# A four-layer gated transformer block on one core: the weight strips, router pieces and layer-norm scales of the second expert layer in another order

## The chip, the core and the metric

The kernel runs on one core of one Trainium2 chip. A core has five engines that work side by side and wait for each other through semaphores: TensorE (PE, matrix products), VectorE (DVE), ScalarE (ACT), GpSimd (POOL) and SyncE (SP, which here only starts DMAs). The time is the device time of one launch in microseconds (us). The profile is one execution of the same program with the hardware profiler on.

## What is computed

Input x is 8 sequences of 128 tokens with 128 features, so 1024 tokens. Four layers follow each other; each adds a gated attention and a gated feed-forward part. The change touches the feed-forward part of the second layer (layer 1 in the code), a mixture of 8 experts:

```python
nx = _ln(x, ln_g, ln_b)
probs = softmax(nx @ router_w)                     # 8 experts, the top 2 kept, w normalised
h1 = gelu(einsum('th,ehf->etf', nx, up_W) + up_b)  # H 128, F 512
s0 = gelu(_ln(einsum('etf,efg->etg', h1[[0,4]], spec0_W) + spec0_b, ln0_g, ln0_b))
t1 = gelu(einsum('etf,efg->etg', h1[[1,5]], spec1a_W) + spec1a_b)      # 512 -> 256
s1 = _ln(einsum('etg,egf->etf', t1, spec1b_W) + spec1b_b, ln1_g, ln1_b) # 256 -> 512
s2 = gelu(einsum('etf,efg->etg', h1[[2,6]], spec2_W) + spec2_b)
h2 = h1 with experts 0,4 <- s0; 1,5 <- s1; 2,6 <- s2
out_e = einsum('etf,efh->eth', h2, down_W) + down_b
y = einsum('eth,te->th', out_e, w) + x
```

All 8 experts run on all tokens; the router's weights are multiplied in at the end. Experts 0, 4, 1 and 5 have a layer norm inside; 2 and 6 have an inner product without one; 3 and 7 have none.

## The kernel before

**Numbers.** Every large product is made of three matmuls on split operands: each operand is written as a high part and a low part (value minus high part), and the product is high times high, high times low, low times high (`mm3`). So every weight and every hidden tile has to be split before TensorE can use it.

**Weights.** SyncE loads a unit's weights into `RAW`. They are split in strips of 128x512 (a `split` piece): VectorE writes the high part `WH` (`high_part`, the CAST in L936), then GpSimd writes the low part `WL` (`low_part`, L607). An expert has one strip for its up weights, four for its inner weights and one for its down weights. TensorE waits for the last strip of an area at the first product that uses it. `RAW` holds one expert's weights, so the DMA for the next expert's area starts when the strips that lay there have their low parts.

**Hidden tiles.** A piece `up`, `spec1a`, `spec2` or `turn` ends in one bank of PSUM (128x512). ScalarE reads it twice, into `G` (L750) and into the high part `H1h` or `H2h` (L752); VectorE then writes the low part `H1l` or `H2l` (L1082). There are four slots of `G`.

**Layer norms.** `spec0` (expert 0, 4) and `spec1b` (expert 1, 5) give one token tile each, four tiles to a half of the tokens (h0, h1). VectorE takes the tile's moments out of PSUM (`tile_stats`: BN_STATS L1030, BN_AGGR L1031, variance L1032), GpSimd raises the variance to -0.5 (L617), VectorE writes the scaled tile `SN` (`tile_scale`, L1038). TensorE then transposes `SN` (`turn`, L1499); the first turn of a half waits for all four scales of that half.

**Ring.** Six PSUM banks are used in a ring by all pieces but `down`: TensorE starts a piece when the reader of the piece six before it is through. Two more banks hold the `down` results.

**Router.** The router's work on VectorE is five `route` pieces of small instructions on 128x64 (L960 to L999). ScalarE has one exponential between parts 0 and 1. The result `WGS` is transposed by TensorE (`wgt`), copied by ScalarE into `WGT`, and spread over partitions (`spread`); `weigh` multiplies an expert's output by it (VectorE, L1017), and GpSimd adds it up (L625).

**Order.** `plan()` writes one list of pieces for the layer (`order[1]`), and every engine walks through this one list and does its own part of each piece, strictly in that order. `weave(a, b, c)` interleaves lists, each one step behind the list before it. So a piece's place in the list sets its place in the queue of VectorE, of GpSimd and of TensorE at once; an engine that waits for one piece does none of the later ones. In the list of before, a layer-norm expert's six strips for the next expert stand in its layer-norm phases (`new[:4]` and `new[4:]` for expert 0 and 4, `new[:3]` and `new[3:]` for 1 and 5), the five router pieces stand in expert 0's second half, and expert 0's `wgt` and `spread` pieces stand behind its down products. A scale stands one piece behind its moments, and the last scale of a half directly behind its moments.

## Time and profile before

| | |
|---|---|
| median of 3 runs | 790.73 us (788.05 to 791.43) |
| span of the profiled execution, first to last instruction | 791.2 us |
| its own time | not listed apart from the span |
| mean granted TensorE clock | 0.922 of full speed |
| the second layer's experts in the span | about 203 to 516 us |
| share of TensorE in the chain that ended last | 70% |

The page gives, for one execution, each engine's busy time, the waits and what ended them, and a timeline. A wait on TensorE is shown in brackets behind the instruction that ended it. PEclk is the granted clock: 1.00 stands for 2.4 GHz, 0.50 for 1.2 GHz. Line numbers are those of the kernel before.

### The profile page before, as it was taken

The numbers are of one execution on the slowest core, as the hardware profiler recorded it, in microseconds if no ns is written. First come the engines' busy times: TensorE is split into PE (matmuls) and PEld (weight loads), VectorE is DVE, ScalarE is ACT, GpSimd is POOL, SyncE is SP. The second block draws the span as 40 slices with busy tenths as digits, with TensorE's granted clock in tenths as the row PEclk, the third lists the DMA queues.
The fourth block names the chain that finished last, engine by engine and source line by source line (L and its number), as shares of the span: only waits on it lengthen the run. The fifth ranks groups of instructions, "written<-read, shape, count | busy, mean of one in ns | idle before, by whom it ended". The sixth has DMA issues, their size and how long they took to land.

```text
span 791.2 us, 10027 instructions
## 1 busy us (share of the span) xinstructions
PE 700.5 (89%) x3468; PEld 547.8 (69%) x3475; DVE 553.0 (70%) x1242; ACT 367.5 (46%) x647; POOL 209.9 (27%) x193
## 2 busy tenths in 40 slices
PE   5989997999898998797999797993759999789997
PEld 2779983889666766675777586771546888567775
DVE  4688766788578585656667735769874554588996
ACT  2334442434435737455275464721214442486673
POOL 5113107322132041124424311143002220214431
PEclk9589997999799999999999989986879999799999
DMA  5102003000001010202010200030000000001000
GB/s 134 39 27 58 2 4 114 31 1 1 1 14 67 3 38 1 68 0 80 14 68 14 66 1 0 1 97 0 1 0 1 1 1 1 27 27 28 1 1 27
DMA packets 27361, 20.97 MB, mean 27 GB/s; under 512 B 5409, under 2 KB 22571, under 8 KB 27311
## 3 DMA queue, kind: packets, MB, share of 16 engines
q1 hardware_dynamic: 26591, 20.29, 8.7%
q8 instruction: 28, 0.46, 0.3%
q14 instruction: 22, 0.18, 0.1%
q10 hardware_dynamic: 720, 0.04, 0.1%
HBM read 19.80 MB, written 0.52 MB: 26 GB/s over the span
## 4 chain that ended last, share of the span: by engine, by line
PE 70%; DVE 17%; issue 4%; ACT 4%; POOL 3%; DMA 1%; ACTq 0%; DVEq 0%; POOLq 0%
PE PS L1366 61%; PE PS L1563 4%; DVE H2l L1082 2%; PE PS L1448 2%; POOL WL L607 2%; ACT H1h L752 1%; DVE SN L1038 1%; PE PS L1499 1%; ACT G L750 1%; DVE WH L936 1%; DVE XN L910 1%; PE PS L1386 1%; DMA GW<-in_L_gate_T 1%; DVE ST L891 1%; POOL RSTD L617 1%
## 5 line engine op out<-in xcount | busy, mean ns | idle before, releaser
L607 POOL TENSOR_TENSOR WL<-RAW,WH 128x512 fp32r<-128x512 f32 (+2 forms) x76 | 95.4, 1272 | 186.9 <-DVE WH L936 186.9
L1082 DVE TENSOR_TENSOR H2l<-G,H2h 128x512 fp32r<-128x512 f32 x104 | 84.0, 822 | 59.7 <-ACT H2h L752 58.7
L1082 DVE TENSOR_TENSOR H1l<-G,H1h 128x512 fp32r<-128x512 f32 x80 | 63.3, 800 | 28.9 <-ACT H1h L752 28.1
L1366 PE MATMUL PS<-H1h,WH 128*128 128x512 f32 x146 | 60.9, 417 | 8.0 <-DVE H1l L1082 8.0
L750 ACT ACTIVATE G<-PS,UB 128x512 f32<-128x512 f32 x64 | 44.8, 700 | 42.4 <-PE PS L1366 38.1
L1366 PE MATMUL PS<-XTh,WH 128*128 128x512 f32 x128 | 55.3, 432 | 9.8 <-POOL WL L607 5.3
L600 POOL TENSOR_TENSOR RSTD<-VE,MHALF 128x4 f32<-128x4 f32 x18 | 19.3, 1072 | 166.5 <-DVE VE L900 166.5
L1366 PEld LDWEIGHTS PS<-V,ATT 77*128 77x128 f32 x512 | 62.5, 192 | 0.6
L625 POOL TENSOR_TENSOR XT<-XT,YW 128x512 f32<-128x512 f32 x24 | 34.8, 1448 | 106.0 <-DVE YW L1017 106.0
L769 ACT ACTIVATE ATT<-ATT 128x308 f32<-128x308 f32 x64 | 29.4, 460 | 71.3 <-DVE ATT L1152 71.0
L1366 PE MATMUL PS<-V,ATT 77*128 77x9 f32 x512 | 61.3, 247 | 0.0
L1144 DVE TENSOR_REDUCE MX<-PS 128x4 f32<-128x308 f32 x64 | 30.5, 477 | 43.6 <-PE PS L1366 42.9
L1366 PE MATMUL PS<-H1l,WH 128*128 128x512 f32 x146 | 58.6, 401 | 0.0
L1366 PE MATMUL PS<-H1h,WL 128*128 128x512 f32 x146 | 58.4, 400 | 0.0
L1366 PE MATMUL PS<-H2h,WH 128*128 128x512 f32 (+1 forms) x108 | 50.6, 469 | 5.6 <-issue 2.0
L1366 PE MATMUL PS<-XTl,WH 128*128 128x512 f32 x128 | 54.0, 422 | 0.0
L685 ACT ACTIVATE ATT<-PS 77x512 f32<-77x512 f32 (+5 forms) x76 | 38.2, 517 | 33.6 <-PE PS L1734 17.0
L1366 PE MATMUL PS<-XTh,WL 128*128 128x512 f32 x128 | 53.8, 420 | 0.0
L1366 PE MATMUL PS<-BDK,ATT 128*128 128x308 f32 x128 | 49.1, 466 | 1.6 <-issue 1.6
L750 ACT ACTIVATE G<-PS,FB 128x512 f32<-128x512 f32 x64 | 43.3, 698 | 13.9 <-PE PS L1366 13.8
L1366 PE MATMUL PS<-H2h,WL 128*128 128x512 f32 (+1 forms) x108 | 44.0, 408 | 0.0
L1366 PE MATMUL PS<-H2l,WH 128*128 128x512 f32 (+1 forms) x108 | 44.0, 407 | 0.0
(242 smaller groups left out, 1677.8 us busy)
## 6 DMA issues: line engine op xcount, KB each, us to landing
RAW<-in_L_ffn_spec_W SPq DMA_DIRECT2D x4, 1024.0 KB, 5.6
RAW<-in_L_ffn_w SPq DMA_DIRECT2D x16, 256.0 KB, 3.0
RAW<-in_L_ffn_up_W SPq DMA_DIRECT2D x8, 256.0 KB, 2.7
RAW<-in_L_ffn_down_W SPq DMA_DIRECT2D x8, 256.0 KB, 3.6
RAW<-in_L_ffn_spec1a_W SPq DMA_DIRECT2D x2, 512.0 KB, 4.3
RAW<-in_L_ffn_spec1b_W SPq DMA_DIRECT2D x2, 512.0 KB, 5.2
RAW<-in_L_ffn_wg SPq DMA_DIRECT2D x4, 176.0 KB, 2.7
RAW<-in_L_ffn_wu SPq DMA_DIRECT2D x4, 176.0 KB, 2.7
```

The source lines that it names most:

```text
L600: g.tensor_tensor(RSTD[:, c], VE[:, c], MHALF[:, c], ALU.pow).then_inc(rstd_ready, 1)
L607: g.tensor_tensor(lo, RAW[0:r["rows"], r["raw"] + s["c0"]:r["raw"] + s["c1"]], hi.bitcast(fp32), ALU.subtract).then_inc(lo_done, 1)
L617: g.tensor_tensor(RSTD[:, i:i + 1], VE[:, i:i + 1], MHALF[:, 0:1], ALU.pow).then_inc(trstd_ready, 1)
L625: g.tensor_tensor(y, y, YW[:, (d % 2) * HALF:(d % 2 + 1) * HALF], ALU.add).then_inc(y_added, 1)
L685: return s.activation(o, i, ACT.Copy)
L750: last = s.activation(G[:, k % 4, :], bank[:, :], func, bias=bias, scale=scale)
L769: s.activation(group(PB, g), group(SUB, g), ACT.Exp, scale=scale).then_inc(exp_done, 1)
L1082: v.tensor_tensor(lo, full, hi.bitcast(fp32), ALU.subtract).then_inc(split_done, 1)
L1144: v.tensor_reduce(MX[:, (g % 4) * GH:(g % 4 + 1) * GH], bank(g), AX.X, ALU.max).then_inc(max_done, 1)
L1366: return t_.matmul(o, l, r, start=start, stop=stop)
L1448: last = t_.transpose(o[0:rows, t * S:(t + 1) * S], SN[:, h, at:at + rows], ident[:, :])
L1563: last = t_.transpose(PS[3 + g % 3][0:KC, m * S:(m + 1) * S], group(PB, g)[:, m * KC:(m + 1) * KC], ident[:, :])
```

## The change

It does three things, all in the second layer's list and in VectorE's walk through it. (1) In experts 0 and 4 the next expert's strips are taken out of the layer-norm phases: one stays between the halves, two stand in the last turns and first down products, three beside the second half's down products. In experts 1 and 5 the strips that stood among `spec1b` stand before it or behind the turns. (2) Router parts 1 to 3 stand among expert 0's down products, part 4 in expert 1's first phase, and expert 0's `wgt` and `spread` pieces stand in expert 1, behind its `up` pieces and ahead of `spec1b`. (3) VectorE's scale of a tile stands two pieces behind its moments; ahead of the first turn of a half all outstanding scales are done.

```diff
@@ down_of
-        if e == 0 and h == 0:
+        if e == 0 and (h == 0 or layer == 1):
             return g
@@
+    first_weights = [piece("wgt", 1, 0, k, 0) for k in range(2)] + [piece("spread", 1, 0, h, 0) for h in range(2)]
@@ plan, the list of layer 1
         if e % 4 == 0:
-            o += weave(spec("spec0", 0, TH), up(e, 1), new[:4])
+            o += weave(spec("spec0", 0, TH), up(e, 1))
             k = route() if e == 0 else []
-            o += k[0:1]
-            o += weave(spec("spec0", 1, TH), spec("turn", 0, 4, buf=2, hi="act"), new[4:], k[1:])
-            o += weave(spec("turn", 1, 4, buf=3, hi="act"), down(e, 0), nxt[:2])
-            o += weave(nxt[2:], down(e, 1))
+            o += new[:1] + k[0:1]
+            o += weave(spec("spec0", 1, TH), spec("turn", 0, 4, buf=2, hi="act"))
+            o += weave(spec("turn", 1, 4, buf=3, hi="act"), down(e, 0), nxt[:2] + k[1:3], new[1:3])
+            o += weave(nxt[2:], down(e, 1), k[3:4] + new[3:])
         elif e % 4 == 1:
-            o += weave(spec("spec1a", 0, 2, buf=2, hi="act"), up(e, 1), new[:3])
-            o += weave(spec("spec1b", 0, TH), spec("spec1a", 1, 2, buf=3, hi="act"), new[3:])
+            if e == 1:
+                o += weave(spec("spec1a", 0, 2, buf=2, hi="act"), up(e, 1), k[4:] + new[:2]) + first_weights + new[2:4]
+            else:
+                o += weave(spec("spec1a", 0, 2, buf=2, hi="act"), up(e, 1), new[:4])
+            o += weave(spec("spec1b", 0, TH), spec("spec1a", 1, 2, buf=3, hi="act"))
             o += weave(spec("spec1b", 1, TH), spec("turn", 0, 4, buf=2, hi="act"), nxt[:2])
-            o += weave(spec("turn", 1, 4, buf=3, hi="act"), down(e, 0), nxt[2:3])
+            o += weave(spec("turn", 1, 4, buf=3, hi="act"), down(e, 0), nxt[2:3], new[4:])
             o += weave(nxt[3:], down(e, 1))
@@ VectorE's mixture
-                    ready, late = late, []
+                    at_once = kind == "turn" and i == 0
+                    for m in late[:len(late) if at_once else max(0, len(late) - 2)]:
+                        if m is not None:
+                            tile_scale(m)
+                    late = [] if at_once else late[-2:]
+                    late.append(s if kind in ("spec0", "spec1b") else None)
@@
                     elif kind in ("spec0", "spec1b"):
                         tile_stats(s)
-                        late = [s]
-                        if i == TH - 1:
-                            for m in ready:
-                                tile_scale(m)
-                            ready, late = [s], []
                     elif kind == "weigh":
                         weigh(s)
-                    for m in ready:
-                        tile_scale(m)
```

**The last scale of expert 0's second half.** VectorE before, from the moments of tile 3 of h1 (PS7 is its bank) on; `SN<-PS7` is the scale that the first turn of h1 waits for:

```order
L1030 BN_STATS ST<-PS7 128x6
L1031 BN_AGGR MV<-ST 128x2
L1032 TENSOR_SCALAR VE<-MV 128x1
L1038 TENSOR_SCALAR SN<-PS7,MV,RSTD 128x512
L1082 TENSOR_TENSOR H2l<-G,H2h 128x512
L936 CAST WH<-RAW 128x512
```

VectorE now, from the moments of the same tile:

```order
L1035 BN_STATS ST<-PS7 128x6
L1036 BN_AGGR MV<-ST 128x2
L1037 TENSOR_SCALAR VE<-MV 128x1
L1043 TENSOR_SCALAR SN<-PS3,MV,RSTD 128x512
L1092 TENSOR_TENSOR H2l<-G,H2h 128x512 x2
L1043 TENSOR_SCALAR SN<-PS7,MV,RSTD 128x512
L1092 TENSOR_TENSOR H2l<-G,H2h 128x512 x3
```

The scale stood directly behind the variance; now two `H2l` splits (of the turns of h0, tiles 2 and 3) stand between. The line numbers have moved with the code.

**Expert 1's inner strips.** VectorE before, at the end of expert 0's first half and ahead of its second; CAST `WH<-RAW` is a weight strip's high part (here inner strips 0, 1 and 2 of expert 1):

```order
L1082 TENSOR_TENSOR H1l<-G,H1h 128x512
L936 CAST WH<-RAW 128x512
L1082 TENSOR_TENSOR H1l<-G,H1h 128x512
L936 CAST WH<-RAW 128x512 x2
L960 COPY RT_60<-PS4 128x64
L961 TENSOR_REDUCE RM<-RT_60 128x8
L962 TENSOR_TENSOR RT_60<-RT_60,RM 128x64
```

VectorE now, from the split of `up` tile 1 of expert 1 (`H1l`) through the down products' phase; the two casts are inner strips 0 and 1, and `RT` and `RM` are the router's:

```order
L1092 TENSOR_TENSOR H1l<-G,H1h 128x512
L941 CAST WH<-RAW 128x512
L972 TENSOR_REDUCE RM<-RT_60 128x8
L973 RECIPROCAL RM<-RM 128x8
L974 TENSOR_TENSOR RT_60<-RT_60,RM 128x64
L941 CAST WH<-RAW 128x512
L979 TENSOR_REDUCE RM<-RT_60 128x8
L980 TENSOR_TENSOR RT_60<-RT_60,RM 128x64
L981 TENSOR_TENSOR RT_60<-RT_60,REV 128x64
L982 TENSOR_REDUCE RM<-RT_60 128x8
L983 TENSOR_TENSOR RT_60<-RT_60,RM 128x64
L985 SCALAR_TENSOR_TENSOR RT_60<-RT_60 128x64
```

And directly behind it, to the splits of the `spec1a` results (`H2l` x2); the three casts are inner strips 2 and 3 and the down strip:

```order
L1092 TENSOR_TENSOR H1l<-G,H1h 128x512 x2
L979 TENSOR_REDUCE RM<-RT_60 128x8
L980 TENSOR_TENSOR RT_60<-RT_60,RM 128x64
L981 TENSOR_TENSOR RT_60<-RT_60,REV 128x64
L982 TENSOR_REDUCE RM<-RT_60 128x8
L983 TENSOR_TENSOR RT_60<-RT_60,RM 128x64
L941 CAST WH<-RAW 128x512 x3
L1092 TENSOR_TENSOR H2l<-G,H2h 128x512 x2
```

Three inner strips stood in the first half and the fourth in the second, far ahead of `spec1a`; now all four stand between the turns' splits and `spec1a`, behind the split `H1l` of `up` tile 1 of expert 1, and the last two also behind router parts 1 to 3 and two more splits.

**The router's transposes on TensorE.** Before, they stand behind expert 0's last down product (`PS4<-H2h`) and ahead of expert 1's `spec1a` (`PS2<-H1h`):

```order
L1366 MATMUL PS4<-H2h,WH 128x512
L1366 MATMUL PS4<-H2l,WH 128x512
L1366 MATMUL PS4<-H2h,WL 128x512
L1366 MATMUL PS6<-identb,WGS_50 96x128 x4
L1366 MATMUL PS7<-identb,WGS_50 96x128 x4
L1366 MATMUL PS0<-WGT,PICK 128x512
L1366 MATMUL PS1<-WGT,PICK 128x512
L1366 MATMUL PS2<-H1h,WH 128x512
L1366 MATMUL PS2<-H1l,WH 128x512
```

Now they stand behind expert 1's last `up` product of h1 (`XTh`) and ahead of `spec1b` (`ROWr`):

```order
L1369 MATMUL PS3<-XTh,WH 128x512
L1369 MATMUL PS3<-XTl,WH 128x512
L1369 MATMUL PS3<-XTh,WL 128x512
L1369 MATMUL PS6<-identb,WGS_50 96x128 x4
L1369 MATMUL PS7<-identb,WGS_50 96x128 x4
L1369 MATMUL PS0<-WGT,PICK 128x512
L1369 MATMUL PS1<-WGT,PICK 128x512
L1369 MATMUL PS2<-ROWr,onesr 128x512
L1369 MATMUL PS2<-WH,H2h 128x512
```

The eight transposes and the two spreads have moved behind two `spec1a` and four `up` pieces.

## Rows read from the trace of the kernel before

**Rows 1.** page part 1: busy time, share of the span, instructions.
```profile
PE 700.5 (89%) x3468; PEld 547.8 (69%) x3475; DVE 553.0 (70%) x1242; ACT 367.5 (46%) x647; POOL 209.9 (27%) x193
```

**Rows 2.** waits inside 203 to 516 us: total, times, longest.
```profile
PE PS L1499 <- DVE SN L1038: 10.4, 6, 2.4
...
PE PS L1366 <- issue: 2.0, 1, 2.0
...
PE PS L1366 <- DVE SN L1038: 1.2, 2, 0.6
...
DVE SN L1038 <- POOL RSTD L617: 8.4, 12, 0.9
...
PE PS L1366 <- POOL WL L607: 3.7, 1, 3.7
```

**Rows 3.** timeline, expert 0 between its turns: start, duration, what.
```profile
245.21 0.70 DVE L1030 BATCH_NORM_STATS2 ST<-PS 128x6 f32<-128x512 f32 x1 [0.16 <-PE PS L1366]
...
246.98 0.81 DVE L1038 TENSOR_SCALAR SN<-PS,MV,RSTD 128x512 f32<-128x512 f32 x1 [0.66 <-POOL RSTD L617]
...
247.65 0.79 ACT L752 ACTIVATE H2h<-PS,LB,LG 128x512 fp32r<-128x512 f32 x1
247.71 0.68 DVE L1082 TENSOR_TENSOR H2l<-G,H2h 128x512 fp32r<-128x512 f32 x1
...
247.84 1.09 PE L1499 MATMUL PS<-ident,SN 128*128 128x128 f32 x8 [1.79 <-DVE SN L1038]
248.30 0.42 DVE L936 CAST WH<-RAW 128x512 fp32r<-128x512 f32 x1
```

**Rows 4.** timeline of all engines, expert 4's turns and down products.
```profile
405.35 1.09 PE L1499 MATMUL PS<-ident,SN 128*128 128x128 f32 x8 [1.80 <-DVE SN L1038]
...
406.04 0.78 ACT L750 ACTIVATE G<-PS,LB,LG 128x512 f32<-128x512 f32 x1
...
413.07 0.75 ACT L752 ACTIVATE H1h<-PS,UB 128x512 fp32r<-128x512 f32 x1
...
415.83 0.80 ACT L752 ACTIVATE H1h<-PS,UB 128x512 fp32r<-128x512 f32 x1
415.99 0.39 PE L1366 MATMUL PS<-H1h,WH 128*128 128x512 f32 x1
```

**Rows 5.** timeline, VectorE's router pieces after expert 0's second half.
```profile
250.81 0.21 DVE L974 TENSOR_REDUCE RM<-RT 128x8 f32<-128x64 f32 x1
...
253.64 0.23 DVE L982 TENSOR_TENSOR RT<-RT 128x64 f32<-128x64 f32 x1
...
256.44 0.22 DVE L999 TENSOR_TENSOR WGS<-RT,WGS 128x64 bf16<-128x64 f32 x1
```

**Rows 6.** timeline, one VectorE split and two GpSimd splits that overlap VectorE's.
```profile
274.17 1.29 POOL L607 TENSOR_TENSOR WL<-RAW,WH 128x512 fp32r<-128x512 f32 x1 [24.08 <-DVE WH L936]
274.22 1.78 DVE L1082 TENSOR_TENSOR H1l<-G,H1h 128x512 fp32r<-128x512 f32 x1
...
276.42 1.67 POOL L607 TENSOR_TENSOR WL<-RAW,WH 128x512 fp32r<-128x512 f32 x1 [0.97 <-DVE WH L936]
```

**Rows 7.** timeline, router products and expert 1's first products.
```profile
261.79 0.61 PE L1366 MATMUL PS<-identb,WGS 128*96 128x128 bf16 x8
...
263.35 0.60 PE L1366 MATMUL PS<-WGT,PICK 96*128 96x512 bf16 x2 [0.95 <-ACT WGT L685]
...
263.60 0.59 PE L1366 MATMUL PS<-H1h,WH 128*128 128x512 f32 x1
...
272.15 0.50 PE L1366 MATMUL PS<-ROWr,onesr 33*128 33x512 f32 x1
...
273.06 0.69 DVE L1082 TENSOR_TENSOR H1l<-G,H1h 128x512 fp32r<-128x512 f32 x1 [0.36 <-ACT H1h L752]
```

**Rows 8.** busy PE, PEld, DVE, ACT, POOL, then PEclk, in one window.
```profile
257.90:261.30 3.40, 3.40 (x10) 2.64 (x9) 2.61 (x5) 3.40 (x7) 0.00 (x0) 0.50 0.00 0
```

**Rows 9.** DMA issues: tensor, count, size, median us from issue to landing.
```profile
RAW<-in_L_ffn_spec_W SPq DMA_DIRECT2D x4, 1024.0 KB, 5.6
```

## The prediction

> **What bounds the kernel now.** I read four views. Part 1 of the page comes first: TensorE is busy for 700.5 us of 791.2 [rows 1], so time is made or lost where TensorE waits, and the question for each moved piece is whether TensorE reaches it before it is ready. Second come the waits between 203 and 516 us, the stretch of the second layer's experts. Those that the change can touch: TensorE waits for a scaled tile `SN`, 10.4 us in 6 waits ahead of transposes and 1.2 us in 2 ahead of products, 2.0 us under "issue" ahead of a down product [rows 2], and 0.95 us for `WGT` [rows 7]. Together 14.5 us. The reader should also see how little GpSimd's power costs: VectorE waits for `RSTD` 8.4 us in 12 waits, 0.9 at most [rows 2]. And one row speaks against the change: once in this stretch TensorE waits 3.7 us for a low part `WL` [rows 2]. That is where a strip stands shortly ahead of its use. Third, the timeline around the places that move gives the durations [rows 3 to 7]. Fourth, the windows give the clock: behind a wait of 2 us, TensorE ran at 0.50 of full speed, the lower level of 1.2 GHz, for 3.4 us [rows 8].
>
> **How I work it out.** All engines walk one list in order. So I take the point at which TensorE starts a marked piece before, walk the new order of VectorE, ScalarE and GpSimd up to what it waits for, with the durations of the rows, and compare the starts. The sum is made against the profiled execution: span 791.2 us, with nothing listed around it; the median of the runs, 790.73, is 0.5 below it, which is within their spread (788.05 to 791.43).
>
> **Part 3 of the change, the scale (both experts 0 and 4).** Before, the first turn of h1 starts at 247.84, when the `SN` started at 246.98 is through, after a wait of 1.79 [rows 3]. The scale now stands behind the `H2l` of turn tile 3 of h0. Its high part on ScalarE ends at 247.65 + 0.79 = 248.44; `H2l` takes 0.6 from start to start (247.71 to 248.30 [rows 3]); the scale takes 0.81; a hand-over about 0.05. TensorE starts at 249.93: **2.1 us later**. Expert 4 has the same shape (a wait of 1.80 [rows 4]) and gets the same 2.1. A gain is excluded here, since ScalarE's pace does not change. ScalarE, which does two passes over each of the next eight tiles, sets the pace of all that follows, so the 2.1 carries on.
>
> **Part 1, expert 1's inner strips.** ScalarE's run over four turns and four `up` tiles, with one spread copy of about 0.5, can be read undisturbed in expert 4: it starts 0.69 behind TensorE (405.35, 406.04), has `up` tile 1 at 413.82 and `up` tile 3 at 416.63 [rows 4]. In expert 0 it would start at 249.93 + 0.7 = 250.6 and, with no spread copy, have tile 1 at 250.6 + 7.8 = 258.4. VectorE's `H1l` of tile 1 ends at 259.0. Only then come, in VectorE's queue: cast, router part 1 (3 instructions), cast, part 2 (6), two `H1l`, part 3 (5), two casts. The eleven instructions of parts 2 and 3 took 2.83 us (250.81 to 253.64 [rows 5]), so 0.26 each and 3.6 for 14; a cast lasts 0.42 [rows 3], taken as 0.35 since the next start overlaps its end as it does the split's (0.68 against 0.6); with 4 casts (1.4) and 2 splits (1.2) that is 6.2 us. Meanwhile GpSimd makes the low parts of strips 0 and 1, 1.29 us each, and VectorE's instruction beside one is held up: an `H1l` that started 0.05 behind a `WL` took 1.78 instead of 0.69, and a `WL` behind a VectorE instruction 1.67 instead of 1.29 [rows 6]. I take 1.9 us for two such hold-ups. The last cast is through at 267.1, and two low parts follow, 2 x 1.29: `spec1a` can start at **269.7**. TensorE would be there at 249.93 + 10.3 = 260.2 (405.35 to 415.99 is 10.6 with two spreads [rows 4]), so it waits 9.5 us for `WL`. Before, `spec1a` started at 263.60 [rows 7]: **+6.1 us**, with the 2.1 above inside. Bounds: +4.2 if the two engines never held each other up, +7 if they did at each strip. The 2.0 under "issue" and the clock loss behind it at 258 us are gone in this, since the new chain does not run through them.
>
 By it, strips are cheap beside a layer norm, whose moments and scales read PSUM, and dear beside the `H1l` and `H2l` splits, which is where they go now. Without it this part would be +4.2 and the one below for expert 4 +7.0.
>
> **Part 2, router part 4 and the transposes.** Before, VectorE's `H1l` of `up` tile 1 of h1 starts 9.46 behind the start of `spec1a` (263.60, 273.06 [rows 7]). Now: 269.7 + 9.46 = 279.2, plus 0.6; then router part 4, which took 253.64 to 256.66, 3.0 us [rows 5]: `WGS` at 282.8. TensorE gets there 8.55 behind `spec1a` (263.60 to 272.15 [rows 7]), at 278.3, and waits 4.5. Transposes, ScalarE's copies and spreads took 261.79 to 263.60, 1.81 us [rows 7]; they stay as they were and now come here. `spec1b` starts at 282.8 + 1.8 = 284.6 instead of 272.15: **+12.5 us in all** so far. Its bounds follow those of the part before, +10.6 to +13.4. The 0.95 for `WGT` is not saved: it stands inside the 1.81.
>
> **Parts 1 and 3 in experts 1 and 5.** Strips leave `spec1b`'s stretch, and one TensorE wait of 0.6 for `SN` goes [rows 2]. But the last scale of h0, which was made during tile 0 of h1, now stands behind the moments of tile 1 of h1, the last product before the first turn: moments 1.1 (245.21 to 246.98 less the 0.66 idle [rows 3]), scale 0.8, hand-overs 0.2, a new wait of about 2.1. The longest wait of all, 2.4 ahead of h1's first turn [rows 2], stays, since an `H1l` and an `H2l` from ScalarE still stand ahead of the scale. Net **+1.5 us in each**, bounds +0.9 to +2.5.
>
> **Part 1, expert 5's inner strips.** Here no router stands between. TensorE starts h1's first turn at 407.45; ScalarE ends `up` tile 1 at 413.82 + 2.1 = 415.9 and tile 3 at 416.63 + 2.1 = 418.7. Strips 0 and 1 are cast at 416.6 to 417.2. GpSimd's first low part holds up the `H1l` of tile 2 until 418.5, its second (from 419.1) that of tile 3 until 420.4; behind it stands the addition of expert 4's weighted output (same shape, 1.29), 421.0 to 422.3, which holds up the casts of strips 2 and 3; two low parts and a third cast between them end at about 425.9. `spec1a` started at 415.99 [rows 4]: **+9.9 us**. Without any hold-up the low parts end at 423.0: +7.0. TensorE is there at 418.1 and waits 7.8.
>
> **Sum.** 12.5 + 1.5 + 9.9 + 1.5 = 25.4. The clock comes on top. A stretch like that of [rows 8] costs 3.4 x (1 - 0.5) = 1.7 us of product time. Waits of 9.5, 4.5 and 7.8 us are new; the waits of 2 us and more in experts 1 and 5 were there before in kind. The slow stretch behind 4.5 us may partly run beside the copy that TensorE waits for. I take 2 of 3, +3.4; bounds 0 and +8 (five stretches). Forecast: 791.2 + 28.8 = **820 us**. Low end: 816.6 without the clock, less 4.8 for hold-ups that don't happen (1.9 and 2.9), less 0.6 in each of experts 1 and 5: 811. High end: 816.6 + 0.9 for hold-ups + 2 for experts 1 and 5 + 8 for the clock: 828. With a little for what I add wrongly, 808 to 830.
>
> **Rivals.**
> 1. *The strips come in time* (the low parts are ready when TensorE gets to `spec1a`). For: POOL is busy for 209.9 us of 791.2, 27% [rows 1], so it has room. Against: it is not POOL's load but its place in the list, behind ScalarE's eighth tile. Then 9.5 and 7.8 us go: 25.4 - 17.3 = 8.1, with one slow stretch 9.8: 801 us. It decides if VectorE reaches inner strip 2 before 257.5. 7%.
> 2. *The ten waits close* (faster). If all 14.5 us [rows 2, 7] went and with them a slow stretch of 1.7 at three of them, it would be 791.2 - 19.6 = 772 us. It decides if the last scale is ready when TensorE ends its two turns, 0.7 us behind the last product; but scale and moments alone take 1.9, so even the best order can't do that with these neighbours. 4%.
> 3. *RAW comes late.* Expert 2's inner load waits for expert 1's last low part, now at 269.7, and lands 5.6 later [rows 9], 275.3; its first cast stands behind router part 4, after 282.8. It is hidden by 7 us, in expert 6 by some 5. If a load took twice 5.6 and more the time would be 835. 4%.
>
> **How the numbers follow.** The forecast has 85%. What a measurement of this kernel can tell from no change is about 0.5%, 4 us. Rival 2 gives nearly all of faster, 4%; within 0.5% lies only a mixture in which strips come in time and some waits close, 2%; slower has the rest, 94%. The range leaves out rivals 1 to 3.
>
> **What would show it.** In the profile after, TensorE waits for POOL `WL` at two new places, about 9 and 8 us long, ahead of `spec1a` of experts 1 and 5; a wait for VectorE's `WGS` of some 4 us ahead of the 8 small transposes; the waits ahead of the first turn of h1 in experts 0 and 4 near 3.9 instead of 1.8; a new wait near 2.1 ahead of the first turn of h0 in experts 1 and 5; more windows at 0.50. From the third expert to the fifth and from the seventh to the end the distances are unchanged. The prediction is wrong if `spec1a` of expert 1 starts less than 4 us later than 263.60, or if the long waits are there and the span still grows by less than 15 us.

## The result and the profile after

| | before | after |
|---|---|---|
| median | 791.08 us (788.05 to 793.03, 4 runs) | 824.28 us (823.88 to 825.33, 4 runs) |
| span of the profiled execution | 791.2 us | 822.2 us, its own time 823.88 |
| mean granted clock | 0.922 | 0.905 |
| first `XM` transpose to last turn back | 315.8 us | 349.4 us |
| from there to the end of the span | 275.7 us | 275.0 us |

The change makes the kernel slower: the ratio is 1.0412, with a 95% interval of 1.0379 to 1.0444, or +32.6 us. 820 us had been forecast. Of the experiments below, e5 and e6 each had one run far outside the others (3667 and 1331 us), which is left out. The last two lines of the table put all of it into the second layer's experts. They are counted on TensorE from its first transpose of `XM`, ahead of the first expert (199.72 before, 197.79 after), to its transpose of `XT` behind the last one (515.55, 547.22), and I call that stretch the stage. Because it starts 1.93 us earlier after the change, differences of places are given below with 1.93 added.

The waits of TensorE in the stage (total, times, longest) answer to [rows 2]. This is after:

```profile
POOL WL L612 <- DVE WH L941: 117.0, 24, 15.1
...
PE PS L1369 <- POOL WL L612: 17.8, 3, 8.4
PE PS L1502 <- DVE SN L1043: 17.2, 8, 3.9
...
PE PS L1369 <- DVE H1l L1092: 7.9, 4, 3.5
...
PE PS L1369 <- DVE WGS L1004: 4.5, 1, 4.5
...
PE PS L1369 <- ACT WGT L690: 0.7, 1, 0.7
```

Waits for `WL` have grown from 3.7 to 17.8 us, those for `SN` from 11.6 (10.4 + 1.2) to 17.2, and the wait for `WGS` is new. "issue" is gone. With all other waits of TensorE in the stage this is 54 us against 32. GpSimd itself waits 117 us for the high parts `WH`, 92.5 before: it is not short of time, it gets its work late.

The places of these waits on TensorE's timeline after the change (start, duration, what, and in brackets the wait ahead of it):

```profile
247.83 1.09 PE L1502 MATMUL PS<-ident,SN 128*128 128x128 f32 x8 [3.89 <-DVE SN L1043]
...
268.12 0.80 PE L1369 MATMUL PS<-H1h,WH 128*128 128x512 f32 x1 [8.41 <-POOL WL L612]
...
283.48 1.09 PE L1369 MATMUL PS<-identb,WGS 128*96 128x128 bf16 x8 [4.52 <-DVE WGS L1004]
...
285.31 1.04 PE L1369 MATMUL PS<-WGT,PICK 96*128 96x512 bf16 x2 [0.74 <-ACT WGT L690]
286.27 0.79 PE L1369 MATMUL PS<-ROWr,onesr 33*128 33x512 f32 x1
...
307.47 0.66 PE L1502 MATMUL PS<-ident,SN 128*128 128x128 f32 x4 [1.92 <-DVE SN L1043]
...
424.41 1.97 PE L1502 MATMUL PS<-ident,SN 128*128 128x128 f32 x8 [3.89 <-DVE SN L1043]
...
443.56 0.79 PE L1369 MATMUL PS<-H1h,WH 128*128 128x512 f32 x1 [5.71 <-POOL WL L612]
```

And all engines between the split of `up` tile 1 and expert 1's first `spec1a`, after the change:

```profile
256.87 0.69 DVE L1092 TENSOR_TENSOR H1l<-G,H1h 128x512 fp32r<-128x512 f32 x1 [0.46 <-ACT H1h L757]
...
257.98 1.29 POOL L612 TENSOR_TENSOR WL<-RAW,WH 128x512 fp32r<-128x512 f32 x1 [13.15 <-DVE WH L941]
...
258.30 1.05 DVE L974 TENSOR_TENSOR RT<-RT,RM 128x64 f32<-128x64 f32 x1
...
259.73 0.21 DVE L979 TENSOR_REDUCE RM<-RT 128x8 f32<-128x64 f32 x1
259.89 1.26 POOL L612 TENSOR_TENSOR WL<-RAW,WH 128x512 fp32r<-128x512 f32 x1 [0.62 <-DVE WH L941]
259.98 1.26 DVE L980 TENSOR_TENSOR RT<-RT,RM 128x64 f32<-128x64 f32 x1
...
262.30 1.29 DVE L1092 TENSOR_TENSOR H1l<-G,H1h 128x512 fp32r<-128x512 f32 x2
...
264.79 2.16 DVE L941 CAST WH<-RAW 128x512 fp32r<-128x512 f32 x3
265.30 4.01 POOL L612 TENSOR_TENSOR WL<-RAW,WH 128x512 fp32r<-128x512 f32 x3 [4.14 <-DVE WH L941]
```

This is the queue that the prediction walked: split, cast, router, cast, router, two splits, router, casts. GpSimd had nothing to do for 13.15 us, gets one strip at 257.98 and the last ones behind 265.30, and TensorE starts at 268.12.

The clock, by windows (stretch, us, then busy time of PE, PEld, DVE, ACT and POOL, then PEclk, the DMA engines' share and their GB/s). Before, the whole stage:

```profile
199.72:515.55 315.83, 283.52 (x1173) 211.51 (x1171) 206.97 (x425) 167.84 (x266) 85.07 (x80) 0.95 0.09 27
```

After, the whole stage, one window behind the first turn of h1 in expert 0, three around `spec1a` of expert 1 and one behind the first turn of h1 in expert 4:

```profile
197.79:547.22 349.43, 295.06 (x1173) 219.61 (x1172) 213.17 (x425) 167.84 (x266) 86.39 (x80) 0.90 0.08 25
...
249.90:253.30 3.40, 3.40 (x16) 2.90 (x14) 2.00 (x3) 2.98 (x6) 0.00 (x0) 0.61 0.00 0
...
263.60:267.00 3.40, 0.00 (x0) 0.00 (x0) 3.18 (x8) 0.00 (x0) 1.71 (x2) 0.50 0.00 0
267.00:270.40 3.40, 2.27 (x5) 1.83 (x6) 0.00 (x0) 0.00 (x0) 2.30 (x2) 0.50 0.18 34
270.40:273.80 3.40, 3.40 (x11) 2.67 (x10) 0.00 (x0) 0.35 (x1) 0.00 (x0) 0.61 0.96 350
...
424.00:427.40 3.40, 2.99 (x11) 2.65 (x12) 0.71 (x2) 1.83 (x3) 0.00 (x0) 0.50 0.00 0
```

TensorE is busy 11.5 us longer with the same 1173 matmuls. So 33.6 us of stage are 22.1 us of waits and 11.5 us of busy time; that the latter is the lower clock, 1.2 GHz, is tested in e7. Around `spec1a` the first of the three windows costs nothing, since no product runs in it; the other two hold 5.7 us of products.

### The profile page after: what moved, and what is told of

It reads as the page before. It is cut to its first block, busy times and chain, and to the rows that moved or that the text cites. A ratio compares the mean times of both kernels' runs of the same rounds, so it can differ in the third digit from the quotient of the medians.

```text
span 822.2 us, 10034 instructions
## 1 busy us (share of the span) xinstructions
PE 708.1 (86%) x3475; PEld 553.2 (67%) x3475; DVE 558.9 (68%) x1242; ACT 366.7 (45%) x647; POOL 211.3 (26%) x193
## 4 chain that ended last, share of the span: by engine, by line
PE 72%; DVE 17%; issue 4%; ACT 4%; POOL 2%; DMA 1%; ACTq 0%; DVEq 0%; POOLq 0%
PE PS L1369 63%; PE PS L1566 3%; PE PS L1502 2%; DVE H2l L1092 2%; PE PS L1451 2%; ACT H1h L757 2%; ACT G L755 1%; DVE WH L941 1%; POOL WL L612 1%; DVE H1l L1092 1%; DVE XN L915 1%; DVE ST L896 1%; PE PS L1389 1%; DMA GW<-in_L_gate_T 1%; DVE QS L1207 1%
## 5 line engine op out<-in xcount | busy, mean ns | idle before, releaser
L1369 PE MATMUL PS<-H1h,WH 128*128 128x512 f32 x146 | 63.3, 434 | 22.1 <-POOL WL L612 14.1
L1369 PE MATMUL PS<-H1l,WH 128*128 128x512 f32 x146 | 60.5, 414 | 0.0
L1147 DVE TENSOR_REDUCE MX<-PS 128x4 f32<-128x308 f32 x64 | 30.5, 477 | 43.8 <-PE PS L1369 43.2
L755 ACT ACTIVATE G<-PS,SB 128x512 f32<-128x512 f32 x24 | 16.5, 689 | 84.6 <-PE PS L1369 84.6
L690 ACT ACTIVATE ATT<-PS 77x512 f32<-77x512 f32 (+5 forms) x76 | 38.1, 517 | 33.7 <-PE PS L1737 18.4
L1369 PEld LDWEIGHTS PS<-H1h,WH 128*128 128x128 f32 x146 | 29.5, 202 | 30.7 <-POOL WL L612 15.0
```

The lines of the kernel that those rows point to most:

```text
L690: return s.activation(o, i, ACT.Copy)
L755: last = s.activation(G[:, k % 4, :], bank[:, :], func, bias=bias, scale=scale)
L1147: v.tensor_reduce(MX[:, (g % 4) * GH:(g % 4 + 1) * GH], bank(g), AX.X, ALU.max).then_inc(max_done, 1)
L1369: return t_.matmul(o, l, r, start=start, stop=stop)
```

## The experiments

My theory: the time goes because a strip's place in the one list puts its cast behind ScalarE's eighth tile and behind the router on VectorE, so TensorE waits for low parts; the scale and the router's transposes add smaller waits, and clock comes on top. The rivals were that the strips alone make nearly all of the loss, that GpSimd's pace counts rather than the place in the list, that the clock does it rather than the waits, and that no order of these pieces could gain. Eleven kernels ran. Each ratio is to executions of the kernel before that ran beside it; "us" in the table is the ratio's distance from 1 times 791.1. Medians of different kernels are compared across such groups, so where they and the ratios differ, both are given.

| kernel | median, runs | ratio (95%) | us | stage in its trace |
|---|---|---|---|---|
| e1_strips | 802.31 (4) | 1.0133 (1.0095 to 1.0170) | +10.5 | 326.5 |
| e2_scale | 790.65 (10) | 0.9972 (0.9943 to 1.0001) | -2.2 | 313.6 |
| e3_router | 793.45 (10) | 1.0027 (1.0004 to 1.0050) | +2.1 | 320.6 |
| e4_no_strips | 797.75 (6) | 1.0060 (1.0025 to 1.0096) | +4.7 | 323.7 |
| e5_strips_ahead | 804.08 (3) | 1.0203 (1.0099 to 1.0308) | +16.1 | 329.1 |
| e6_narrow_low | 819.23 (3) | 1.0385 (1.0294 to 1.0477) | +30.5 | 342.7 |
| e7_keep_after | 816.31 (4) | 1.0345 (1.0280 to 1.0411) | +27.3 | 341.0 |
| e8_keep_before | 787.36 (12) | 0.9960 (0.9925 to 0.9994) | -3.2 | 306.8 |
| e9_scale_keep | 783.59 (6) | 0.9877 (0.9832 to 0.9921) | -9.7 | 308.1 |
| e10_other_order | 788.19 (12) | 0.9934 (0.9906 to 0.9962) | -5.2 | 313.5 |
| e11_order_keep | 778.03 (6) | 0.9806 (0.9757 to 0.9854) | -15.3 | 306.3 |

### One part at a time: e1, e2, e3, and two parts: e4

e1 is the kernel before with the strips moved as in the change, the router and the scale as they were:

```diff
-            o += weave(spec("spec0", 0, TH), up(e, 1), new[:4])
+            o += weave(spec("spec0", 0, TH), up(e, 1))
-            o += k[0:1]
-            o += weave(spec("spec0", 1, TH), spec("turn", 0, 4, buf=2, hi="act"), new[4:], k[1:])
-            o += weave(spec("turn", 1, 4, buf=3, hi="act"), down(e, 0), nxt[:2])
-            o += weave(nxt[2:], down(e, 1))
+            o += new[:1] + k[0:1]
+            o += weave(spec("spec0", 1, TH), spec("turn", 0, 4, buf=2, hi="act"), [], k[1:])
+            o += weave(spec("turn", 1, 4, buf=3, hi="act"), down(e, 0), nxt[:2], new[1:3])
+            o += weave(nxt[2:], down(e, 1), new[3:])
```

and for experts 1 and 5 `new[:4]` ahead of `spec1b` and `new[4:]` with the turns.

> Only part 1: the strips stand where the changed kernel has them; router pieces and scales as before. Walking theory (what counts is what stands ahead of the last inner strip in VectorE's queue): in expert 1 no router pieces stand between the strips, so TensorE waits about 5 us for WL ahead of spec1a instead of 8.4, in expert 5 about 6 to 8 as in the changed kernel; with a slow clock stretch or two, +11 to +15 us, 802 to 806. Rival A (the strips' place alone is the whole cost): +28 to +33. Rival B (the cost is mostly the scale and the router): under +5.

Measured: +10.5 us. The trace of e1, TensorE:

```profile
251.59 1.09 PE L1499 MATMUL PS<-ident,SN 128*128 128x128 f32 x8 [1.79 <-DVE SN L1038]
...
270.55 0.79 PE L1366 MATMUL PS<-H1h,WH 128*128 128x512 f32 x1 [3.63 <-POOL WL L607]
...
430.04 0.80 PE L1366 MATMUL PS<-H1h,WH 128*128 128x512 f32 x1 [6.74 <-POOL WL L607]
```

The strips alone make both new waits for `WL`, and the turn's wait stays as in [rows 3]. Ahead of expert 1 the wait is 3.63 where the whole change has 8.41. Counted from the stage's start, `spec1a` starts at 67.4 in e1 and at 70.3 after the change, so 2.9 of these 4.8 us are strips that come sooner: 1.6 because the turn ahead of them starts sooner (48.4 against 50.0) and 1.3 behind it. The other 1.9 us are no gain: TensorE itself arrives later, since the router's transposes and spreads still stand ahead of `spec1a`. It is a little less than I had expected, and the rival that the strips make nearly all of the loss by themselves falls.

e2 is the kernel before with only the scale's new rule, the last two blocks of the change's diff:

```diff
-                    ready, late = late, []
+                    at_once = kind == "turn" and i == 0
+                    for m in late[:len(late) if at_once else max(0, len(late) - 2)]:
+                        if m is not None:
+                            tile_scale(m)
+                    late = [] if at_once else late[-2:]
```

> Only part 3: scales two pieces behind the moments; strips and router as before. Theory: the wait ahead of the first turn of h1 grows from 1.8 to about 3 in experts 0 and 4, less than the 3.9 of the changed kernel since VectorE is still held by strips there; expert 0's 2.0 us wait for the down product shrinks in return; +2 to +5 us, 793 to 796. Rival (the parts add up one by one): 2 x 2.1 + 2 x 1.5 = +7.2, 798.

Measured: no change that can be told, -2.2 us with an interval that reaches 1.0001. The turns of h1 wait 2.89 us, as expected, but the total misses: the waits for `SN` are 11.3 against 11.6 us and all waits of the stage are the same, because "issue" 2.0 is gone and the small ones elsewhere have changed places. I had priced a longer wait and not what it takes over.

e3 is the kernel before with only the router pieces, `wgt` and `spread` moved:

```diff
-            o += weave(spec("spec0", 1, TH), spec("turn", 0, 4, buf=2, hi="act"), new[4:], k[1:])
-            o += weave(spec("turn", 1, 4, buf=3, hi="act"), down(e, 0), nxt[:2])
-            o += weave(nxt[2:], down(e, 1))
+            o += weave(spec("spec0", 1, TH), spec("turn", 0, 4, buf=2, hi="act"), new[4:])
+            o += weave(spec("turn", 1, 4, buf=3, hi="act"), down(e, 0), nxt[:2] + k[1:3])
+            o += weave(nxt[2:], down(e, 1), k[3:4])
+            if e == 1:
+                o += weave(spec("spec1a", 0, 2, buf=2, hi="act"), up(e, 1), k[4:] + new[:3]) + first_weights
```

> Only part 2: router pieces spread over experts 0 and 1, transposes ahead of spec1b; strips and scales as before. Theory: the 2.0 us wait goes and a wait of about 4.4 us for WGS comes, +1 to +4 us, 792 to 795. Rival (the router pieces are the cost wherever the strips stand): +8 or more.

Measured: +2.1 us, as expected. The wait for `WGS` is there at its full size, less the 2.0 us of "issue" that it replaces:

```profile
274.98 1.09 PE L1371 MATMUL PS<-identb,WGS 128*96 128x128 bf16 x8 [4.52 <-DVE WGS L1004]
```

e4 has the edits of e2 and e3 together, the strips as before.

> Parts 2 and 3 together, strips as before. Theory: no wait for WL ahead of spec1a in experts 1 and 5 beyond 1 us; the waits for WGS (4.4) and for the scales remain; +5 to +9 us, 796 to 800, so that putting the strips back gives 24 to 28 of the 33 us. Rival (strips, router and scale each add a fixed amount): this run is e2 plus e3 and the changed kernel is e1 plus e2 plus e3.

Measured: +4.7 us, just under what I had expected, where e2 and e3 add up to -0.1. Between e4 and the change lie only the strips, and they cost 27.9 us there (32.6 - 4.7), against 10.5 on top of the kernel before. The parts add up to 10.5 - 2.2 + 2.1 = 10.4 us, the change costs 32.6. So 22 us belong to no part alone. In TensorE's waits of the stage for `SN`, `WL`, `WGS`, `WGT`, `H1l` and "issue" it is e1 +7.5, e2 0, e3 +2.8 and all three +21.9: half of the 22 is in waits. One piece of that is 8.41 against 3.63 above. Another is the scale. VectorE after the change, ahead of the first turn of h1:

```profile
245.02 0.69 DVE L1092 TENSOR_TENSOR H2l<-G,H2h 128x512 fp32r<-128x512 f32 x1
...
246.36 0.69 DVE L1092 TENSOR_TENSOR H2l<-G,H2h 128x512 fp32r<-128x512 f32 x1 [0.65 <-ACT H2h L757]
246.97 0.81 DVE L1043 TENSOR_SCALAR SN<-PS,MV,RSTD 128x512 f32<-128x512 f32 x1
```

and the same place in e2:

```profile
244.07 0.69 DVE L1087 TENSOR_TENSOR H2l<-G,H2h 128x512 fp32r<-128x512 f32 x1 [0.81 <-ACT H2h L752]
244.68 0.42 DVE L936 CAST WH<-RAW 128x512 fp32r<-128x512 f32 x1
245.01 0.81 DVE L1038 TENSOR_SCALAR SN<-PS,MV,RSTD 128x512 f32<-128x512 f32 x1
```

The rule waits for two pieces of VectorE's list, and a strip is a piece. With strips among the tiles, two pieces are one split and one cast; with the strips taken out, they are two splits, and the second waits for ScalarE. That is 3.89 against 2.89 us, and by the same counting it is why the 1.92 us ahead of the first turn of h0 in experts 1 and 5 stands in the change and not in e2, whose 11.3 us are two of 2.89, two of 2.49 and two of 0.3.

### The strips' place: e5

e5 is the changed kernel with the inner strips put ahead of the second half's turns and of router parts 1 to 3; parts 1 and 2 come somewhat later by this, and the wait for `WGS` stays as it was:

```diff
-            o += weave(spec("turn", 1, 4, buf=3, hi="act"), down(e, 0), nxt[:2] + k[1:3], new[1:3])
-            o += weave(nxt[2:], down(e, 1), k[3:4] + new[3:])
+            o += new[1:5] + weave(spec("turn", 1, 4, buf=3, hi="act"), down(e, 0), nxt[:2])
+            o += weave(nxt[2:], down(e, 1), k[1:4] + new[5:])
```

> The changed kernel with one thing moved: the four inner strips of expert 1 (and 5) stand directly ahead of the first turn of h1, ahead of the router pieces and of the turns' splits; still outside the layer norm's products. Theory (it is the place behind ScalarE's tiles and the router pieces that costs): no wait for WL ahead of spec1a above 1 us; the waits of 3.9 and 4.5 stay; about +8 in waits and a little clock over the kernel before, 799 to 804. Rival (strips are dear anywhere beside the splits, through the hold-ups between GpSimd and VectorE): above 812.

Measured: +16.1 us, the ratio's interval +8 to +24; its median, 804.08, lies at the upper edge of my range, and +16.1 would be 807. The waits of TensorE:

```profile
PE PS L1502 <- DVE SN L1043: 17.2, 8, 3.9
PE PS L1369 <- DVE H1l L1092: 7.9, 4, 3.5
PE PS L1369 <- POOL WL L612: 4.7, 3, 3.7
PE PS L1369 <- DVE WGS L1004: 4.5, 1, 4.5
```

Only the waits for `WL` differ from the change's, 4.7 against 17.8 us, and half of the loss is gone. The same strips, scale and router are done. The stage is 20.3 us shorter than the change's: 12.9 in waits and 7.4 in TensorE's busy time (287.7 against 295.1). So the place alone cost about 16 us, give or take 9 by the intervals, waits and clock together.

### GpSimd's share: e6

e6 is the changed kernel with a narrow low part: of the inner strips of experts 1 and 5 only 64 of 512 columns are computed. The rest holds zeros for expert 1 (one memset ahead of the layer) and, for expert 5, what an earlier expert left there. So a part of the low products is left out of the result.

```diff
-                hi, lo = weights(r, s["c0"], s["c1"])
+                c1 = s["c0"] + 64 if r["kind"] == "inner" and r["unit"] in (E0P + 1, E0P + 5) else s["c1"]
+                hi, lo = weights(r, s["c0"], c1)
```

> The changed kernel, but GpSimd makes only 64 of 512 columns of the low part in the eight inner strips of experts 1 and 5 (the rest is left out, so the products there are not the reference's), and fills expert 1's part with zeros once ahead of the layer. Theory: the low parts cost twice, by 2 x 1.29 at the end of the queue and by hold-ups of about 2 us each; the wait ahead of spec1a falls from 8.4 to about 4.5 in expert 1 and from 5.7 to about 2 in expert 5; 814 to 818. Rival (no hold-ups, only the two last low parts count): the waits fall by 2.0 each, 819 to 821. Rival (VectorE's queue alone): unchanged, 824.

Measured: the waits ahead of `spec1a` go from 8.41 to 4.75 and from 5.71 to 2.68:

```profile
267.46 0.79 PE L1372 MATMUL PS<-H1h,WH 128*128 128x512 f32 x1 [4.75 <-POOL WL L613]
...
439.09 0.79 PE L1372 MATMUL PS<-H1h,WH 128*128 128x512 f32 x1 [2.68 <-POOL WL L613]
```

So the last low parts and their hold-ups of VectorE are 3.7 and 3.0 us of these waits; the rest is VectorE's and ScalarE's queue. In time I had expected 814 to 818 and the median is 819.23; the interval overlaps the change's, so the gain is read from the trace alone. The trace also has a wait of 1.8 us for `XM` near the stage's start, 0.3 after the change, which takes back a part of it.

### The clock: e7, e8, e9

e7 is the changed kernel with useless matmuls ahead of its waits (bf16, 128x512, into a bank of the ring that the next piece overwrites), so that TensorE stays at work while it waits:

```diff
+                FILL = {('turn', 0, 1): 14, ('turn', 4, 1): 14, ('spec1a', 1, 0): 30, ('spec1a', 5, 0): 24,
+                        ('wgt', 0, 0): 16, ('turn', 1, 0): 6, ('turn', 5, 0): 6, ('turn', 1, 1): 8, ('turn', 5, 1): 8}
+                def fill(o, s):
+                    for _ in range(FILL.get((s["kind"], s["e"], s["h"]), 0) if s["i"] == 0 else 0):
+                        mm(o[:, :], identb[:, :], MB1[:, 0:HALF])
```

> The changed kernel with idle TensorE time filled: matmuls of bf16 128x512 into the bank that is written next, ahead of each wait that the change made or left in experts 0, 1, 4, 5 (14 and 14 ahead of the first turns of h1 in experts 0 and 4, 30 and 24 ahead of spec1a, 16 ahead of the router's transposes, 6 and 8 ahead of the turns of experts 1 and 5), fewer than fit into the wait. Theory (about 10 of the 33 us are TensorE's lower clock behind the waits, not waits): 813 to 819, with the waits in the trace filled and few windows at 0.50 between 245 and 320. Rival (the clock costs nothing, since other engines set the pace behind each wait): 822 to 826, or more.

Measured: 816.31, 8.0 us below the change. The stage, then a piece of the filling ahead of expert 1's `spec1a`, and the first products of `spec1a` and `spec1b`:

```profile
201.71:542.68 340.97, 309.69 (x1293) 221.86 (x1298) 212.85 (x423) 167.03 (x266) 85.90 (x80) 0.95 0.08 25
```

```profile
267.76 1.24 PE L1369 MATMUL PS<-MB,identb 128*128 128x512 bf16 x5
271.95 0.50 PE L1369 MATMUL PS<-H1h,WH 128*128 128x512 f32 x1 [2.95 <-POOL WL L612]
...
287.14 0.50 PE L1369 MATMUL PS<-ROWr,onesr 33*128 33x512 f32 x1
```

PEclk is 0.95, as in the kernel before, where the change had 0.90. A filling matmul takes (1.24 - 0.38) / 4 = 0.215 us from start to start, so 126 of them are 27 us, and 309.7 - 27 = 282.6 us are left for the real ones: 12.5 less than in the change, about what the kernel before needs (283.5). Waits and filling together are 58.4 us against 54.4: since TensorE arrives sooner, it waits longer. So the clock costs the change 12.5 us of work, of which 4 are hidden in waits: 8.5 us net in the stage and 8.0 by the medians. By the ratios it is 5.3 us (27.3 against 32.6), with intervals that overlap, so the size is known only roughly. Nothing that TensorE waits for comes sooner by this, and the loss that is left, 25 us by the medians and 27 by e7's own ratio, is the waits'.

e8 is the kernel before, filled in the same way:

```diff
+                FILL = {('turn', 0, 1): 5, ('turn', 4, 1): 5, ('turn', 1, 1): 8, ('turn', 5, 1): 8,
+                        ('spec2', 2, 1): 12, ('spec2', 6, 1): 12, ('up', 4, 0): 13}
```

> The kernel before with the same filling: 5 matmuls ahead of the first turn of h1 in experts 0 and 4, 8 in experts 1 and 5, 12 inside the second half's first spec2 product of experts 2 and 6, 13 ahead of expert 4's first up product. Theory: five of its slow stretches in this layer (1.7 us each) go: 781 to 787. Rival (clock costs nothing): 791 to 794.

Measured: -3.2 us, a little above my range. Its trace, the stage's stretch and the one behind it:

```profile
203.00:505.00 302.00, 285.69 (x1222) 208.72 (x1227) 203.43 (x408) 163.69 (x263) 83.57 (x79) 0.98 0.09 29
505.00:781.00 276.00, 235.37 (x1222) 184.68 (x1226) 201.87 (x425) 120.75 (x228) 67.78 (x44) 0.89 0.05 15
```

The stage is 9.0 us shorter, with PEclk at 0.98; behind it nothing is won. This execution (783.31 us) is among the fastest of twelve, so the median gains less than its trace shows, and where the rest goes in the other executions I can't tell.

e9 is e2 with e8's filling but for:

```diff
-('turn', 0, 1): 5, ('turn', 4, 1): 5
+('turn', 0, 1): 9, ('turn', 4, 1): 9
```

> The kernel before with the change's scale part alone (as e2) and with the filling of e8, 9 matmuls ahead of the first turn of h1 in experts 0 and 4 since the wait there is 2.9. Theory: e2's and e8's gains stand beside each other in part, 782 to 788, below both kernels. Rival (e2's gain was fewer slow stretches by chance of where they fall, so that with filling nothing of it is left): the same as e8, 787 or more.

Measured: 783.59, -9.7 us, as expected. The later scale does no harm when its wait is filled. That it is faster than e8 can't be put down to the scale: its filling ahead of those turns is also longer, and in the traces its stage is no shorter (308.1 against 306.8 us). Where that difference comes from is open.

### Another order: e10, e11

e10 keeps the change's router and `wgt` idea but in experts 0 and 4 leaves the strips where they are early: four in the first layer-norm half as before and the rest in the second, with one `up` piece of the next expert behind them. Router parts 1 to 3 stand beside expert 0's last down products, part 4 in expert 1's first phase, `wgt` and `spread` behind `spec1b` of h0. Experts 1 and 5 have the strips where the change has them, and the scale is as before:

```diff
-            o += weave(spec("spec0", 1, TH), spec("turn", 0, 4, buf=2, hi="act"), new[4:], k[1:])
-            o += weave(spec("turn", 1, 4, buf=3, hi="act"), down(e, 0), nxt[:2])
-            o += weave(nxt[2:], down(e, 1))
+            o += weave(spec("spec0", 1, TH), spec("turn", 0, 4, buf=2, hi="act"), new[4:] + nxt[:1])
+            o += weave(spec("turn", 1, 4, buf=3, hi="act"), down(e, 0), nxt[1:2])
+            o += weave(nxt[2:], down(e, 1), [], k[1:4])
...
-            o += weave(spec("spec1b", 0, TH), spec("spec1a", 1, 2, buf=3, hi="act"), new[3:])
+            o += weave(spec("spec1b", 0, TH), spec("spec1a", 1, 2, buf=3, hi="act")) + (first_weights if e == 1 else [])
```

> Another order, made from what the waits show: experts 0 and 4 keep the strips in the layer-norm phases but two up products of the next expert stand among the turns of h0 and h1, router parts 1 to 3 stand behind the second half's down products, part 4 behind expert 1's second up product, the transposes and spreads behind spec1b's first half; experts 1 and 5 have the change's strip places; scales as before. Theory: expert 0's 2.0 and 0.95 waits and 1.4 of experts 1's and 5's go, the first turns of h1 wait 1.1 to 1.4: 785 to 789. Rival (what is saved comes back as waits for WGT): 790 to 793.

Measured: 788.19, -5.2 us, as expected. Its waits for `SN` and `WL`:

```profile
PE PS L1501 <- DVE SN L1040: 6.3, 4, 2.3
PE PS L1368 <- POOL WL L609: 5.0, 3, 3.7
...
PE PS L1368 <- DVE SN L1040: 1.7, 2, 1.4
```

The wait ahead of the first turn of h1 in expert 0 is 1.09 instead of 1.79 us, "issue" and the wait for `WGS` are gone, and the one price seen is 1.36 us for a scale ahead of a spread, in the last row. So an order of these pieces can gain, but by 5 us and not by closing the ten waits.

e11 is e10 with e8's filling but for:

```diff
-('turn', 0, 1): 5, ('turn', 4, 1): 5
+('turn', 0, 1): 3, ('turn', 4, 1): 3
```

> e10 with filling: 3 matmuls ahead of the first turns of h1 in experts 0 and 4, 8 in experts 1 and 5, 12 in experts 2 and 6, 13 ahead of expert 4. Theory: 780 to 785, the fastest of all. Rival (TensorE's clock in the next layer gives the gain back, as part of it went in e8): 785 to 788.

Measured: 778.03 us (771.48 to 785.03), by its ratio 15 us below the kernel before, and some 46 below the change, the fastest of all. It is somewhat better than I had expected, and its stage, 306.3 us, is about e8's; what it wins over e8 beyond that lies outside the stage and isn't explained.

## Why the prediction was right, and where its sizes were off

The time (820 forecast, 824.28 measured, in the range of 808 to 830), the sign and the mechanism held. Step by step, with the marks moved by 1.93:

- **The scale.** Forecast: the first turn of h1 2.1 us later, a wait of 3.9. Measured: 1.92 us later (247.83 + 1.93 against 247.84), and waits of 3.89 in both experts. This step stands only beside part 1; in e2 the wait is 2.89. I had walked the order of the whole change, so I got the right number without saying that it depends on the strips.
- **Expert 1's inner strips.** Forecast +6.1 at `spec1a`, a wait of 9.5. Measured +6.45 (263.60 to 268.12 + 1.93) and 8.41. The two hold-ups cost (1.05 - 0.23) + (1.26 - 0.23) = 1.9 us, as taken, but fell on two router instructions and not on splits. The wait is shorter since TensorE itself came 1.4 us later than forecast (268.12 - 8.41 = 259.71, against 260.2 - 1.93): the stretch at 249.9 with PEclk 0.61, behind the turn's new wait, lay on its way and not on VectorE's.
- **Router part 4 and the transposes.** Forecast a wait of 4.5 for `WGS`: measured 4.52. The whole step was forecast at +12.5 and came to +16.05. The 3.5 us are the clock: behind `spec1a` TensorE ran 5.7 us at 0.50 and 0.61, and the transposes and spreads took 2.79 us (283.48 to 286.27) instead of 1.81. e7 bears this out: with the waits filled, `spec1a` is as late as in the change (+6.4), but `spec1b` only by 13.0 us (287.14 - 201.71, against 272.15 - 199.72).
- **Experts 1 and 5.** Forecast a new wait of about 2.1 ahead of the first turn of h0: measured 1.92 in expert 1 and 1.91 in expert 5. The wait ahead of h1's stayed at 2.5. The net was forecast at +1.5; from `spec1b` to the first turn of h1 expert 1 took 31.60 us (286.27 to 317.87) instead of 29.09, +2.5, the upper bound.
- **Expert 5's inner strips.** Forecast a wait of 7.8, measured 5.71, for the same reason. From the turn of h1 to `spec1a` it was to be 18.4 us (407.45 to 425.9) and was 19.15 (424.41 to 443.56), so the strips came nearly as forecast; TensorE needed 13.4 us to get there instead of 10.6.
- **Sum without the clock.** Forecast 25.4. e7, in which the clock is back at the level of before, has a stage 25.1 us longer and a median of 816.31, where the text had 816.6 without the clock. By e7's own ratio it is +27.3. So this sum was about right, but that it is met to 0.3 us is partly luck, since its steps miss in both directions. Against the kernel before, e7 is 15.3 us late at expert 1's second spread (14.0 forecast), 26.2 at expert 5's `spec1a` (23.9) and 24.3 at expert 5's second spread (25.4). And e7 isn't the change without new slow stretches only: it also fills waits of 2.4 us in experts 1 and 5 that the kernel before has unfilled.
- **The clock, the term that was mis-sized.** Forecast +3.4, two stretches, bounds 0 and +8. Measured with e7: 8.5 us net in the stage and 8.0 by the medians, at the upper bound, and 5.3 by the ratios. What failed is the count: I had looked for slow stretches only behind the three longest waits. They also stand behind waits of 3.89 (249.9, 424.0) and others, and the one of 8.41 left 5.7 us of products at 0.50 and 0.61 (267.0 to 273.8), where I had taken 3.4.
- **Rivals.** Strips in time (801 us): e5 makes them so, and the time is 804; in the change they are not. The ten waits closing (772): no order that ran did so; e10 gains 5.2. A late `RAW`: the waits for `WL` are three, two at the new places and the old one of 3.7. Its 835 us had no working: by the prediction's own numbers a load of twice 5.6 us would land at 280.9, still ahead of the first cast at 282.8.

What I had not seen is how the parts hang together: 10.4 us singly, 32.6 together. The router alone costs 2.1 us and the scale alone nothing that can be told, yet they stand in the same queue as the strips. By the traces some half of the 22 us is in waits, as above (21.9 against 7.5 + 0 + 2.8); the other half is TensorE's busy time, which in the stage rows is +2.7 us in e1 (286.2 busy), -2.3 in e2 (281.2), +1.5 in e3 (285.0) and +11.5 in all three. My reading, argued and not tested part by part, is that more waits in one stage, each longer, leave more of it slow.

The Trainium skill, "SBUF — State Buffer", "Who interferes with whom", says that a VectorE instruction with two SBUF inputs contends with a GpSimd instruction that reads SBUF, and that the ports they share are locked exclusively. The trace agrees down to 128x64: a two-input instruction that takes 0.23 us alone took 1.05 and 1.26 beside a low part. A reduction of the router that lies wholly inside another low part (232.23, the low part from 232.14 for 1.28 us) kept its 0.22.

## What to carry to other kernels

Where all engines walk one list, put work that a reader waits for (here the last of four strips) ahead of pieces that wait for another engine; the place alone was worth about 16 us. Parts of such an edit don't add, so walk the order of the whole, and look at what a rule counted in pieces becomes when pieces move away. Count the lower clock behind every new wait, and where a long one can't be closed, try useless matmuls in it: they gave 8 us after the change (5 by the ratios), 3 before it and 10 on top of the better order.

## What the runs showed of the hardware

- A 128x64 VectorE instruction that takes 0.23 us [rows 5] took 1.05 and 1.26 us beside a GpSimd low part of 1.29 and 1.26. Both ended 0.1 us behind the low part (259.35 against 259.27, 261.24 against 261.15): what they cost was set by what was left of GpSimd's instruction, not by their own length.
- Filling waits of 1.8 to 8.4 us with bf16 matmuls raised PEclk of the stage from 0.90 to 0.95 after the change and from 0.95 to 0.98 before it. Part of what that gives is returned as longer waits (4 of 12.5 us in e7).
- The stretch behind the stage took 275.0 us after the change and 275.7 before it: a stage 33.6 us longer left nothing for the next one.
